# mLSTM heads issued by pairs, four weight and decay buffers, a filler product per pair, and the finish of a batch spread out

## What is computed

```python
logfg = log_sigmoid(f_pre)
Fcum = cumsum(logfg)
Dmat = Fcum[..., :, None] - Fcum[..., None, :] + i_pre[..., None, :]
Dmat = where(causal, Dmat, -inf)
m = max(Dmat, axis=-1)
Smat = exp(Dmat - m)                       # the "decay"
qk = einsum('bhsd,bhtd->bhst', q, k) / sqrt(dqk)
C = qk * Smat                              # the "weights"
n = maximum(abs(sum(C, -1)), exp(-m))
h = einsum('bhst,bhtd->bhsd', C / n, v)
# then: RMS norm per head, times sigmoid(output gate), output projection, residual
```

## Time and profile before

| | us |
|---|---|
| median of three runs | 750.72 |
| the profiled execution | 753.29 |
| its span | 751.5 |
| PE busy in the span | 712.5 |
| DVE busy | 443.5 |
| ACT busy | 423.5 |
| POOL busy | 252.0 |
| mean granted TensorE clock | 0.935 |

### The profile page before, as it was taken

How to read it: one execution, slowest core, us unless ns; L and a number is a source line. 1 busy time by engine, 2 the same in 40 slices (tenths; PEclk the granted TensorE clock), 3 DMA queues, 4 the chain that set the end, 5 groups by cost and what they waited for, 6 DMA issues and landing times. The chain is left out here.

```text
span 751.5 us, 15356 instructions
## 1 busy us (share of the span) xinstructions
PE 712.5 (95%) x5290; PEld 670.3 (89%) x5290; DVE 443.5 (59%) x961; ACT 423.5 (56%) x1106; POOL 252.0 (34%) x265
## 2 busy tenths in 40 slices
PE   8999999999999999999987999988998799999995
PEld 8999999999999999999877999987666579999995
DVE  6465665576655766566565655643155437655686
ACT  5566686667756677666684333366454544333553
POOL 3624742244422434224741411217254122111011
PEclk9999999999999999999999999998556659999998
DMA  6266644456343663436500400007320100000000
GB/s 228 72 209 196 174 131 123 119 167 176 118 119 100 181 181 102 131 96 185 169 3 4 159 2 0 15 11 235 113 69 15 44 0 1 2 0 0 1 28 28
DMA packets 44889, 69.63 MB, mean 93 GB/s; under 512 B 3376, under 2 KB 30640, under 8 KB 44592
## 3 DMA queue, kind: packets, MB, share of 16 engines
q1 hardware_dynamic: 44416, 68.31, 30.4%
q10 hardware_dynamic: 432, 0.79, 0.3%
HBM read 52.18 MB, written 16.91 MB: 92 GB/s over the span
## 5 line engine op out<-in xcount | busy, mean ns | idle before, releaser
L303 PE MATMUL PJ<-xTh,WBh 128*128 128x256 f32 x364 | 106.6, 293 | 0.4 <-POOL WBl L808 0.4
L305 PE MATMUL PJ<-xTh,WBl 128*128 128x256 f32 x364 | 102.7, 282 | 0.0
L304 PE MATMUL PJ<-xTl,WBh 128*128 128x256 f32 x364 | 102.7, 282 | 0.0
L545 ACT ACTIVATE probs<-SC,nmax 128x256 f32<-128x256 f32 x128 | 59.5, 471 | 63.9 <-DVE nmax L671 62.4
L793 POOL TENSOR_TENSOR stage<-stage 128x256 f32<-128x256 f32 x32 | 24.5, 765 | 164.1 <-DVE stage L659 164.1
L669 DVE TENSOR_REDUCE rmax<-SC 128x2 f32<-128x512 f32 x64 | 44.2, 691 | 54.4 <-PE SC L384 47.5
L1154 PE MATMUL UG<-xTh,WBh 128*128 (+1 forms) x256 | 73.5, 287 | 1.1 <-PEq L49 1.1
L552 ACT ACTIVATE probs<-probs,rinv 128x256 f32<-128x256 f32 x128 | 58.5, 509 | 27.2 <-DVE rinv L675 27.1
L1157 PE MATMUL UG<-xTh,WBl 128*128 (+1 forms) x256 | 72.4, 283 | 0.0
L1155 PE MATMUL UG<-xTl,WBh 128*128 (+1 forms) x256 | 72.4, 283 | 0.0
L303 PEld LDWEIGHTS PJ<-xTh,WBh 128*128 128x128 f32 x364 | 69.2, 190 | 1.0 <-issue 0.6
(11 more groups left out here) (252 smaller groups left out, 2453.4 us busy)
## 6 DMA issues: line engine op xcount, KB each, us to landing
K<-scr_k SPq DMA_DIRECT2D x60, 256.0 KB, 4.5
raw<-in_w_att SPq DMA_DIRECT2D x37, 256.0 KB, 4.7
Q<-scr_q SPq DMA_DIRECT2D x15, 512.0 KB, 7.4
stage<-scr_m SPq DMA_DIRECT2D x4, 1024.0 KB, 5.9
scr_q<-rot_h SPq DMA_DIRECT2D x30, 128.0 KB
scr_q<-rot_l SPq DMA_DIRECT2D x30, 128.0 KB
scr_k<-rot_h SPq DMA_DIRECT2D x30, 128.0 KB
scr_k<-rot_l SPq DMA_DIRECT2D x30, 128.0 KB
```

What stands on the lines that cost most here:

```text
L303: pe.matmul(out, ah, bh, start=(i == 0), stop=False)
L304: pe.matmul(out, ah, bl, start=False, stop=False)
L305: last = pe.matmul(out, al, bh, start=False, stop=(i == n - 1))
L545: last = act.activation(probs[:, j % 2, t, :], SC[j % 2][:, t, :], ACT.Exp, scale=SCALE, bias=nmax[:, j % 2, t:t + 1], accum_out=rsum[:, j ...
```

## The change

- **Pairs.** `heads(c)` goes through four pairs. Each issues both scores of the next pair (at the end of a batch those of the next batch's first), a filler product, both values, and one `back`. The scores still alternate between two banks.
- **Four buffers.** The two halves of `ga` and `gb` are joined by four pieces of a tile `rows` of 6 x 256 columns, which also holds cumS, gr, nm, ones and M, no longer needed by then. Weights and decays wait for the head four back.
- **The filler** `busy(c, pair)`: one product of 128x128 weights with 128x512 weights into the bank TB. Its result is not used. It is left out once (batch 3, pair 1), where TB holds a norm transpose.
- **Start.** The gate sigmoid is computed as tanh(x/2), with the factor (1 + tanh) in `norm_b` and 4 in the norm's constants; the `ACT_TABLE_LOAD` in front of the first gate and that in front of exp(-m) are gone from ScalarE's list. `rows_T` moves ahead of the last projection, exp(-m) ahead of the last q and k, the first four decays around the last gate. Batch 0's mask is added by VectorE in four pieces (`mask_first`, 128x512 each), GpSimd adds those of batches 1 to 3.
- **Finish.** heads_T, hoT, project_out and add_heads of batch c move from batch c + 1 to c + 2, the norm's transpose and split from c + 2 to c + 3; those of batches 2 and 3 go into the first MLP batch, and the last norm into the second, for which `chunks` unrolls one more batch (`finish_last`).
- **Weights.** The MLP pieces 5 to 11 are converted in batch 0 (2, 2, 2, 1 a pair); their loads all stand ahead of the rows of batch 2 in SyncE's list.

The diff, cut to its core:

```diff
-        cumS, gr, M, nm, ones = (sb(n, [P, S]) for n in ("cumS", "gr", "M", "nm", "ones"))
+        rows = sb("rows", [P, 6 * S])
+        cumS, gr, nm, ones, M = (rows[:, i * S:(i + 1) * S] for i in range(5))
+        decay_buf = [ga[:, 0, :], ga[:, 1, :], rows[:, 768:1152], rows[:, 1152:1536]]
+        weight_buf = [gb[:, 0, :], gb[:, 1, :], rows[:, 0:384], rows[:, 384:768]]
...
             def values(c, h):
                 pe.wait_ge(s_["c_ready"], HM * c + h + 1)
+                if c == 0 and h == 0:
+                    pe.wait_ge(s_["og_ready"], TT * B)
...
+            def busy(c, pair):
+                if c == 3 and pair == 1:
+                    return
+                if c == 3 and pair == 2:
+                    pe.wait_ge(s_["xt_split"], N_T[2] + 1)
+                pe.matmul(TB[:, :], WLh[:, 0, 0:P], WLh[:, 1, :], start=True, stop=True)
+
             def heads(c):
-                scores(c, 0)
-                for h in range(HM):
-                    if h + 1 < HM:
-                        scores(c, h + 1)
-                    values(c, h)
...
+                if c == 0:
+                    scores(0, 0)
+                    scores(0, 1)
+                for pair in range(PAIRS):
+                    if pair + 1 < PAIRS:
+                        scores(c, 2 * pair + 2)
+                        scores(c, 2 * pair + 3)
+                    elif c + 1 < B:
+                        scores(c + 1, 0)
+                        scores(c + 1, 1)
+                    busy(c, pair)
+                    values(c, 2 * pair)
+                    values(c, 2 * pair + 1)
+                    if pair:
+                        back(c, pair - 1)
+                    elif c:
+                        back(c - 1, PAIRS - 1)
+                    if pair == 0 and c >= 2:
+                        heads_T(c - 2)
+                    if pair == 0 and c >= 3:
+                        pe_T(pe, 2, c - 3)
+                    if pair == 1 and c >= 2:
+                        project_out(c - 2)
...
             def finish_heads(k, c, ht):
                 if ht == 0:
-                    back(3, 3)
+                    back(3, PAIRS - 1)
+                    heads_T(2)
+                if ht == 1:
+                    project_out(2)
+                    pe_T(pe, 2, 1)
+                if ht == 5:
+                    heads_T(3)
+                if ht == 6:
+                    project_out(3)
+                    pe_T(pe, 2, 2)
+            def finish_last(ht):
                 if ht == 2:
-                    pe_T(pe, 2, 2)
...
+                    pe_T(pe, 2, 3)
...
+            def mask_first(quarter):
+                dve.wait_ge(a_in[0], 32)
+                a = A[0][:, 2 * quarter:2 * quarter + 2, :].rearrange("p h (b n) -> p h b n", n=P)[:, :, 0:3:2, :]
+                m = mask[:, :].rearrange("p (a b n) -> p a b n", a=1, b=1).broadcast_to([P, 2, 2, P])
+                dve.tensor_tensor(a, a, m, ALU.add).then_inc(s_["masked_first"], 1)
...
             for c in range(B):
-                for h in range(HM):
-                    weigh(c, h)
...
+                for pair in range(PAIRS):
+                    weigh(c, 2 * pair)
+                    weigh(c, 2 * pair + 1)
+                    if c == 0 and pair == 0:
+                        mask_first(2)
+                        mask_first(3)
...
+                    if pair == 1 and c:
                         norm_a(c - 1)
+                    if pair == 2 and c >= 2:
+                        add_heads(c - 2)
+                    if pair == 3 and c:
+                        norm_b(c - 1)
```

More of the change, by code:

```diff
@@ L1622, in _ @@
             gates()
[L1623 removed]
+            evac_qk(1)
+            evac_og(1)
             mlp_hi(2, 4)
[L1625 removed]
+            evac_qk(2)
+            evac_og(2)
+            exp_nm()
             mlp_hi(4, 5)
[L1627 to L1636 removed]
+            evac_qk(3)
@@ new lines, in _ @@
+            decay(0, 0)
+            decay(0, 1)
+            evac_og(3)
+            decay(0, 2)
+            decay(0, 3)
+            for c in range(B):
+                for pair in range(PAIRS):
+                    if pair:
+                        take_pair(c, pair - 1)
+                    elif c:
+                        take_pair(c - 1, PAIRS - 1)
+                    if pair == 0 and c >= 2:
+                        hoT(c - 2)
+                    if pair == 0 and c >= 3:
+                        act_hi(act, 2, c - 3)
+                    if pair == 1 and c:
@@ L1649, in _ @@
-            take_pair(3, 3)
+                    if c == 0:
+                        i = RING + sum(MLP_PIECES[:pair])
+                        mlp_hi(i, i + MLP_PIECES[pair])
+                    for u in (HM * c + 2 * pair + 4, HM * c + 2 * pair + 5):
+                        if u < HM * B:
+                            decay(u // HM, u % HM)
+            take_pair(3, PAIRS - 1)
             def finish_heads(k, c, ht):
                 if ht == 0:
+                    hoT(2)
                     take(3)
@@ new lines, in _ @@
+            mask_first(0)
+            take_v(3, 0)
+            mask_first(1)
+            take_v(3, 1)
+            for c in range(B):
+                for pair in range(PAIRS):
+                    weigh(c, 2 * pair)
[3 more added lines that the diff above has]
+                        mask_first(3)
+                    if pair == 0 and c >= 2:
+                        hoT(c - 2)
+                    if pair == 0 and c >= 3:
+                        dve_lo(dve, 2, c - 3)
+                    if pair == 1 and c:
+                        norm_a(c - 1)
+                    if pair == 2 and c >= 2:
+                        add_heads(c - 2)
+                    if pair == 3 and c:
+                        norm_b(c - 1)
+                    if pair == 3 and c >= 2:
+                        dve_xs(dve, 2, c - 2)
@@ L1789, in finish_heads @@
             def finish_heads(k, c, ht):
                 if ht == 0:
+                    hoT(2)
+                if ht == 1:
                     norm_a(3)
+                    dve_lo(dve, 2, 1)
+                if ht == 2:
+                    add_heads(2)
+                if ht == 4:
+                    norm_b(3)
+                if ht == 5:
+                    dve_xs(dve, 2, 2)
+                    hoT(3)
+                if ht == 7:
+                    add_heads(3)
+                    dve_lo(dve, 2, 2)
```

176 lines of the change are left out of this document (68 added, 108 removed).

## The result

| | before | after |
|---|---|---|
| median, us | 750.81 (749.76 to 752.95, 4 runs) | 721.34 (719.29 to 725.06, 4 runs) |
| ratio | | 0.961, 95% interval 0.9565 to 0.9654 |
| the profiled execution, span | 753.29, 751.5 | 720.92, 719.1 |
| mean granted clock | 0.935 | 0.978 |
| first scores to first FFN product | 517.04 to 619.98, 102.9 | 518.16 to 586.07, 67.9 |

A forecast was written before the change was run, and what follows sets the result against it. TensorE at half clock was taken to bound the mLSTM heads; their 102.9 us would become 65.3 (heads) + 2.4 (finish moved to FFN) - 1.3 (waits gone) = 66.4, 36.5 less, giving 714 us, range 702 to 746.

The forecast's parts named there:

- my first case: Whole kernel: clock mostly held through the heads, 714 us (702 to 722), chance 0.50.
- mostly held: Clock in the heads: one filler a pair keeps it up, as the mixture gains full-array work and loses idle.
- 2.53 + 0.23 = 2.76 us a pair: Heads at full clock: a pair's scores, values and back transpose take 2.53 us, the filler product 0.23.
- 3.5 us of waste: Filler in the heads: by the skill's rule that idle alone matters, its 15 x 0.23 us would be wasted.
- 0.8 and 3.0 us of idle: Start of the heads: TensorE idles 0.8 us for first weights, 3.0 (0 to 4.8) where VectorE's masks meet GpSimd's.
- The meeting of batch 3's mask and norm_b: Second batch: GpSimd's mask of batch 3 beside VectorE's norm multiplications of batch 0, 3.5 us idle (0 to 5).
- 0.2 us a pair: Heads: added to each pair (0 to 0.6) for late VectorE norms, head adds and splits, 3.2 us in all.
- 1.0 in batch 0: Batch 0 of the heads: ScalarE also converts seven weight pieces, 1.0 us more.
- Two pairs at half: Heads: each of two idles may drop the clock for one pair, 2.9 us more each, so 5.9.
- The floor of 701 us: Whole kernel: with all bounds of the stalls at zero the sum is 50, some 701 us.
- C: Rival for the clock in the heads: the filler does nothing, half clock as before, 747 us, chance 0.17.
- D: Rival, slower: C, plus shared-port meetings and heavier VectorE lists delaying each next score, 756 us, chance 0.08.

The follow-up runs named there:

- e2: The kernel before with only 14 of the 128x512 products added, one ahead of the values of each even head: 756.62 us, ratio 1.0059 to before.
- e1: The changed kernel without its 15 filler products: 716.2 us, ratio 0.9517 to before.
- e8: The changed kernel without the product and with TensorE head by head again, four buffers and spread finish kept: 739.0 us, ratio 0.9714 to before.
- e9: The kernel before with only TensorE's order changed to pairs, two buffers and lumped finish kept: 761.16 us, ratio 1.0114 to before.
- e7: The changed kernel without the product and with two weight and two decay buffers instead of four: 717.34 us, ratio 0.9551 to before.
- e4: The changed kernel with VectorE's splits of finished work one pair later: 717.55 us, ratio 0.9552 to before.
- e5: The changed kernel without the product and with VectorE's splits of finished work one pair later: 713.14 us, ratio 0.9466 to before.
- e3: The changed kernel with batch 0's mask back on GpSimd, none on VectorE: 720.18 us, ratio 0.9591 to before.
- e12: The changed kernel without product, splits later, all masks on VectorE, ScalarE's copy of finished heads earlier, norm_a one pair later: 708.09 us, ratio 0.9403 to before.
- e6: The changed kernel without the product, splits one pair later, all masks on VectorE: 712.38 us, ratio 0.9463 to before.

## Why the prediction was right, and where it wasn't

I said 714 us; 721.3 was measured, in my range and at the edge of my first case's own (702 to 722). That the clock would be mostly held was right; the reason that I gave for it was wrong, so that much of the hit is luck. By that reason the product alone should have helped, and e2 lost 0.6%. In the profiled executions I had 716.8 and 720.9 came out. The 4.1 us are: the heads 67.9 instead of 65.3, 2.6; what follows them 133.0 us against 131.5 before, 1.5 more instead of 1.1, 0.4; and the first scores 1.1 us later. For the last: both executions have a half-clock stretch of about 3.4 us near 497, which no edit touches; in after it begins about 1 us earlier, at the start of the last gate projections instead of at their end, and TensorE later waits 1.47 us for VectorE instead of 0.51. Over all traces the first scores stand anywhere from 516.1 to 518.6.

- **Why the clock came back: wrong.** "I choose 'mostly held', since the mixture gains full-array work and loses idle." The full-array work did nothing (e1, e2). What my forecast needed was the order, which I had only counted as a rearrangement: head by head the clock can stay at half for 51.2 us without a wait over 1.3 (e8); by pairs it comes back after 3.5 us in the kernel before, as long as no finish is in the way, and stays down for 20.5 and 23.9 us where the lumped finish makes TensorE wait (e9); by pairs with the finish spread it comes back after 3.4 to 13.7 us each time (all the others). Neither edit gives the gain alone: on before's heads of 102.9 us, pairs alone +8.6; the spread finish with four buffers and the new start -14.6; both -40.1 (e1). That the two are worth far more together than apart is shown, though four buffers and the new start are in the second of them and only the buffers were taken out again (e7); what in the order by pairs the chip reacts to (fewer turns between 32-row and 33-column products, or the denser stream) no run here separates.
- **The product's cost: the sum right by two errors.** I took 2.53 + 0.23 = 2.76 us a pair and 2.78 was measured. The pair without it is 2.36, as two heads' values run back to back without a turn between, and the product costs 0.42, as it adds a turn of its own. By the rule of the Trainium skill (TensorE: Matmul & The Clock Gate, What's actually happening: the default is throttled, and activity releases it) I had estimated the product as 3.5 us of waste. That it is waste is right (5.1 us); on the clock this case's traces disagree, if activity means busy time: 49.94 busy of 51.2 us didn't release it in e8.
- **The start: the mechanism right, its size in part luck.** 0.8 and 3.0 us of idle; 0.64 and 3.21 measured. I had one GpSimd addition in VectorE's way. In after both were; where it was one (e1, e4, e5, e7), the idle was 0 to 1.75 us. The Trainium skill (SBUF — State Buffer, Practical consequences) says that whichever engine issues first holds the shared ports for its whole instruction and the other blocks. The rows agree: the earlier trace rows, 5.36 us for two of 0.68 where GpSimd began first, 3.45 where it began second, and 1.44 and 2.27 for 0.18 in e1.
- **The meeting of batch 3's mask and norm_b, 3.5 us: wrong place.** norm_b took 0.76. The mask that matters is batch 2's, with norm_a: 1 us of idle in after, 4.57 to 4.83 in four variants (e1, e3, e4, e7). I had looked for large operations only; a blocked one of 0.18 us lost 2.1.
- **0.2 us a pair, 3.2 in all, and 1.0 in batch 0: wrong form.** No pair has such a gap, and batch 0 doesn't wait for ScalarE. Three waits stand instead, 0.98, 2.30 and 2.65, 5.9 us. The last two are VectorE's split, queued ahead of the weights and waiting for ScalarE (e4). All idle terms together I had at 11.5 us; the heads have 9.8.
- **Two pairs at half: too few.** I had 11.8 us at the half clock and 17.0 were. At about half a us lost for each, that is 2.6 us more; the idle gives 1.7 back, and 1.7 of the heads' miss I can't assign.
- **Four buffers** I counted as the cover for decays that run ahead. In e7's trace they are worth at most 2.5 us.
- **The floor of 701 us** does not follow from its own terms: 50 us of heads with the same +2.4 and -1.3 give 699. Nothing else hangs on it.
- The rivals C and D priced the product at 0.46 us at half; e2 has 0.72, for the same turn that I left out at full clock. Their clock is that of e2 and of e8, not of pairs with a spread finish.

## What to carry to other kernels

Group products of one shape before turning to the other, and take waits out in the same step: here the first alone lost 8.6 us of the heads and the second alone won 14.6 of 40.1. Which of two engines starts first, by a few tenths of a us, moved a wait by up to 3 us here, so look at the traces of several variants before putting a wait down to an edit. Where an engine works in order, put nothing that waits for another engine ahead of what TensorE waits for; one pair later is often free (e4, e12). Do not buy the clock with idle products before a run has shown that they hold it.

## What the runs showed of the hardware

- The granted clock stayed at 0.50 for 51.2 us with TensorE busy 97.5% of them (e8), and for 20.5 us at 100% with full-array products mixed in (e2). The same head products by pairs were back at 1.00 after 3.5 us (e9, batch 0). Being busy was not enough.
- A VectorE operation of 128x16 with two inputs in SBUF took 2.27 us instead of 0.18 beside a GpSimd addition of 2.3 us (e1), so its size gave no protection. Two of 128x512 took 5.36, 3.45 or 1.28 us with two, one or no such additions in the way (after, e1, e6).
- A turn from products of one tile shape to another cost about 0.2 us at full clock: the 128x512 product, itself 0.23, added 0.42 between the 32-row scores and the 33-column values (from the last score's start to the first value's 0.64 us in after, 0.22 in e1).
